# A feature-interaction tower on one core: a new order of whole and split groups, gathers in one row, low parts two groups later, first loads and dense features redone

## The reference

```python
x0 = xk = e
for idx, (W, b) in enumerate([(w0, b0), (w1, b1), (w2, b2)]):
    z = jnp.einsum('bhd,bkd,hks->bsd', x0, xk, W) + b[None, :, None]   # s = 128
    z = jax.nn.relu(z)
    if idx != 2:
        xk = z[:, :64, :]
        direct.append(z[:, 64:, :])
    else:
        direct.append(z)
logit = jnp.sum(jnp.concatenate(direct, axis=1), axis=-1)              # 512 x 256
h = jnp.concatenate([logit, dense_ctx], axis=1)
h = jnp.maximum(h @ W_top1 + b_top1, 0.0)                              # 272 -> 512
h = jnp.maximum(h @ W_top2 + b_top2, 0.0)                              # 512 -> 256
y = h @ W_top3
```

## Time and profile before

| | us |
|---|---|
| median of 3 runs | 640.83 (639.80 to 641.92) |
| profiled execution, its own time | 640.96 |
| its span, first to last instruction | 639.2 |
| mean granted TensorE clock | 0.992 |
| TensorE busy | 608.4 (95%) |
| VectorE busy | 551.1 (86%) |
| ScalarE busy | 302.9 (47%) |
| GpSimd busy | 462.2 (72%) |
| share of the last-ending chain on TensorE | 91% |

### The profile page before, as it was taken

The page is one execution under the profiler, slowest core; times in us unless marked ns, Lnnn a source line. Parts: engine busy times, 40 slices in busy tenths (PEclk is TensorE's granted clock), DMA queues, the critical chain, the costliest instruction groups (busy, mean ns, idle before and its releaser), DMA issues.

```text
span 639.2 us, 7262 instructions
## 1 busy us (share of the span) xinstructions
PE 608.4 (95%) x1938; PEld 364.9 (57%) x1938; DVE 551.1 (86%) x511; ACT 302.9 (47%) x374; POOL 462.2 (72%) x293
## 2 busy tenths in 40 slices
PE   0777999999999999999999999999999999999998
PEld 0334665656666665656666666656566666656463
DVE  1665999999999999999999999999999999999540
ACT  2124546445454545555464546465453545455313
POOL 6827787878878787878788787878788787547230
PEclk9997999999999999999999999999999999999998
DMA  7799697878869494958779594949688694922000
GB/s 252 161 230 221 139 209 153 197 159 188 170 141 219 102 215 95 223 116 202 148 163 201 120 218 99 218 101 218 133 188 165 146 214 97 218 51 70 2 0 0
DMA packets 28415, 98.46 MB, mean 154 GB/s; under 512 B 8017, under 2 KB 16977, under 8 KB 20082
## 3 DMA queue, kind: packets, MB, share of 16 engines
q1 hardware_dynamic: 21544, 93.68, 66.3%
q0 software_dynamic: 5120, 1.32, 1.9%
q10 hardware_dynamic: 1738, 3.33, 1.4%
HBM read 94.47 MB, written 3.84 MB: 154 GB/s over the span
## 4 chain that ended last, share of the span: by engine, by line
PE 91%; POOL 4%; DMA 3%; issue 1%; ACT 0%; SPq 0%; DVE 0%; ACTq 0%
PE z L614 42%; PE z L625 13%; PE z L620 13%; PE z L622 13%; PE z L604 4%; POOL gathered L411 3%; PE z L608 2%; PE z L607 2%; PE d_products L700 1%; DMA gathered<-in_tables,rows_sb 1%; DMA x_rows<-gathered 1%; PE z L675 1%; POOL low L352 0%; PE x_bank L675 0%; PE z L686 0%
## 5 line engine op out<-in xcount | busy, mean ns | idle before, releaser
L352 POOL TENSOR_TENSOR low<-products,high 128x1024 fp32r<-128x1024 f32 x128 | 303.8, 2390 | 110.9 <-ACT high L741 100.1
L465 DVE TENSOR_TENSOR products<-x_rep,xk 128x1024 f32<-128x1024 f32 (+1 forms) x258 | 333.3, 1339 | 24.3 <-ACT xk L725 16.6
L614 PE MATMUL z<-products,w_whole 128*128 128x512 f32 x640 | 296.9, 594 | 0.1
L741 ACT ACTIVATE high<-products 128x1024 fp32r<-128x1024 f32 x128 | 134.9, 1055 | 134.4 <-DVE products L465 121.8
L620 PE MATMUL z<-high,w_high 128*128 128x512 f32 x352 | 183.5, 521 | 6.8 <-ACT high L741 6.8
L411 POOL DMA_INDIRECT gathered<-in_tables,rows_sb x160 | 157.7, 985 | 44.3 <-issue 41.0
L614 PEld LDWEIGHTS z<-products,w_whole 128*128 128x128 f32 x640 | 121.5, 190 | 104.3 <-issue 92.8
L622 PE MATMUL z<-high,w_low 128*128 128x512 f32 x352 | 138.9, 395 | 0.0
L625 PE MATMUL z<-low,w_high 128*128 128x512 f32 x352 | 109.8, 393 | 1.8 <-POOL low L352 1.6
L620 PEld LDWEIGHTS z<-high,w_high 128*128 128x128 f32 x352 | 66.5, 189 | 45.6 <-issue 25.2
L622 PEld LDWEIGHTS z<-high,w_low 128*128 128x128 f32 x352 | 66.6, 189 | 37.0 <-issue 26.3
(11 more groups left out here) (51 smaller groups left out, 176.2 us busy)
## 6 DMA issues: line engine op xcount, KB each, us to landing
x_rep<-x_rows SPq DMA_DIRECT2D x60, 768.0 KB, 15.2
x_rep<-x_rows SPq DMA_DIRECT2D x66, 512.0 KB, 6.5
x_rows<-gathered SPq DMA_DIRECT2D x16, 225.0 KB
x_rep<-in_w ACTq DMA_DIRECT2D x2, 1280.0 KB, 9.6
gathered<-in_tables,rows_sb POOLq DMA_INDIRECT x160
x_rep<-x_rows SPq DMA_DIRECT2D x4, 384.0 KB, 6.3
x_same<-x_rows SPq DMA_DIRECT2D x15, 78.0 KB
x_same<-x_rows SPq DMA_DIRECT2D x16, 64.0 KB
```

The lines of the kernel that those rows point to most:

```text
L352: ops.tensor_tensor(low[0:p, slot, 0:n, :], product(index, p, n), high[0:p, slot, 0:n, :].bitcast(fp32), ALU.subtract).then_inc(low_by[kin ...
L465: nc.vector.tensor_tensor(slots, rep, row.unsqueeze(1).broadcast_to([p, n, N]), ALU.mult).then_inc(made, 1 + pair)
L614: mm = nc.tensor.matmul(out, w_whole[0:p, at, i, :], product(index, p, n)[:, i, :], start=(first and i == 0), stop=(last and i == n - 1))
L741: nc.scalar.activation(high[0:p, slot, 0:n, :], product(index, p, n), ACT.Copy).then_inc(rounded, 1)
```

## The change

- **Kinds.** `KINDS` becomes `ppwpdpwpdh` (layer 1), `wdws` (layer 0), `wwwwpwppwh` (layer 2). Per chunk there are as before 10 w, 8 p, 3 d, 2 h and 1 s. The slots' users follow: groups 0 and 1 now follow groups 19 (w) and 20 (p) in their ring slots, before 18 and 20 (both p); 2 and 3 follow 21 (p) and 22 (w).
- **Gathers.** All ten behind group 15, in layer 2 (before: one behind group 1, nine behind 6).
- **Low lag** 2 for 1.
- **ScalarE's order.** In chunk 0 the copy of x_same stands ahead of layer 0's groups, no longer ahead of group 2; the direct part of layer 2 comes one group later; xk1 (`after_layer1`) is made behind the rounding of groups 11 and 13, before behind that of 11 and 12. VectorE's reductions move by one group.
- **First loads.** Part (6, 10) is cut in two, SP no longer holds parts back until earlier ones have landed (`HELD`), and chunk 1's rows are written to DRAM, after a wait for their gathers, behind part 2 (`WRITTEN_AFTER`) instead of behind part 4. The tiles made by selection are chosen anew.
- **Dense features.** Instead of an fp32 product over 16 partitions, dense rows and their weights are loaded three times, at partitions 0, 32 and 64 of a tile pair that GpSimd has cleared; ScalarE rounds the pair into a free slot of `high`, VectorE puts the rests at partitions 64 and 32, and TensorE does one rounded pass over 128 partitions per block of 128 outputs. The last chunk's ScalarE gets two waits for it.

```diff
-FIRST_PARTS = [(4, 6), (0, 4), (6, 10), (10, 14), (14, 17), (17, T1)]
-SELECTED = [0, 1, 6, 2, 3]
+FIRST_PARTS = [(4, 6), (0, 4), (6, 8), (8, 10), (10, 14), (14, 17), (17, T1)]
+SELECTED = [0, 1, 2, 3, 6]
...
-KINDS = {1: "wpwpwppwdh", 0: "wsdw", 2: "wwpwpdpwph"}
+KINDS = {1: "ppwpdpwpdh", 0: "wdws", 2: "wwwwpwppwh"}
...
-GATHERS = {1: 1, 6: 9}
+GATHERS = {15: 10}
-LOW_LAG = 1
-SEL_SLOT = 0
+LOW_LAG = 2
+SEL_SLOT = 7
...
-        HELD = 3
-        WRITTEN_AFTER = 4
+        WRITTEN_AFTER = 2
...
             for q in range(1, len(FIRST_PARTS)):
-                if q >= HELD:
-                    sp.wait_ge(first_loaded[q - 2], 32)
                 for e in range(2):
                     load_replicated(sp, 0, e, FIRST_PARTS[q], first_loaded[q])
...
+            sp.wait_ge(dense_zeroed, 1)
+            for p in (0, 32, 64):
+                sp.dma_start(dense_rows[p:p + DENSE, 0, :], dense).then_inc(dense_loaded, 16)
+                sp.dma_start(dense_rows[p:p + DENSE, 1, :], wt1[256:256 + DENSE, :]).then_inc(dense_loaded, 16)
...
+                    if index == DENSE_TO and c == C - 2:
+                        pool.wait_ge(made, count("all", c, N1 + N0 + 1))
+                        nc.gpsimd.memset(dense_rows, 0.0).then_inc(dense_zeroed, 1)
...
+            def make_dense():
+                dve.wait_ge(dense_rounded, 1)
+                for i, p in ((0, 64), (1, 32)):
+                    nc.vector.tensor_tensor(dense_parts[p:p + DENSE, i, :], dense_rows[p:p + DENSE, i, :],
+                                            dense_parts[p:p + DENSE, i, :].bitcast(fp32),
+                                            ALU.subtract).then_inc(dense_made, 1)
...
-                nc.tensor.matmul(z_hidden1[m][:, :], wt1d_sb[:, m * 128:(m + 1) * 128], dense_sb,
+                nc.tensor.matmul(z_hidden1[m][:, :], dense_parts[:, 1, m * 128:(m + 1) * 128], dense_parts[:, 0, :],
                                  start=True, stop=False)
...
-                    if index == 2 and not last:
+                    if index == (N1 if first else 2) and not last:
                         copy_same(c + 1)
-                    if index == 3 and not first:
+                    if index == 4 and not first:
                         after_layer2(c - 1, first=isinstance(c, int) and c == 1)
+                    if last and index == N1:
+                        act.wait_ge(dense_loaded, 16 * 6)
+                        act.wait_ge(used, count("all", c, DENSE_FROM))
+                        nc.scalar.activation(dense_parts, dense_rows, ACT.Copy).then_inc(dense_rounded, 1)
-                    if index == N1 + 3:
+                    if index == N1 + 5:
                         after_layer1(c)
```

More of the change, by code:

```diff
@@ L234, in dlrm_cin_kernel @@
         wt1_sb = x0_rep[:, 0:2, 0:H1]
-        wt1d_sb = x0_rep[0:DENSE, 2, 0:H1]
-        dense_sb = x0_rep[0:DENSE, 3, 0:B]
+        dense_rows = x0_rep[:, 2:4, :]
+        dense_slot = next(SPLIT.index(i) % PART_RING for i in SPLIT if i in LAYER0)
+        same_slot = [i for i in SPLIT if SPLIT.index(i) % PART_RING == dense_slot and i not in LAYER0]
+        DENSE_FROM, DENSE_TO = max(i for i in same_slot if i < N1), min(i for i in same_slot if i > N1)
+        dense_parts = high[:, dense_slot, :, :]
         wt2_sb = x0_rep[:, 4:8, 0:H2]
@@ L270, in dlrm_cin_kernel @@
         top_loaded = sem("top_loaded")
+        dense_zeroed, dense_loaded = sem("dense_zeroed"), sem("dense_loaded")
+        dense_rounded, dense_made = sem("dense_rounded"), sem("dense_made")
         same_loaded = sem("same_loaded")
@@ L395, in _ @@
                         load_replicated(sp, c, e, part, rep_loaded[q])
+            sp.wait_ge(dense_zeroed, 1)
+            for p in (0, 32, 64):
+                sp.dma_start(dense_rows[p:p + DENSE, 0, :], dense).then_inc(dense_loaded, 16)
+                sp.dma_start(dense_rows[p:p + DENSE, 1, :], wt1[256:256 + DENSE, :]).then_inc(dense_loaded, 16)
             sp.wait_ge(made, count("all", C - 2, len(BODY) - 1))
-            sp.dma_start(dense_sb, dense).then_inc(top_loaded, 16)
             sp.dma_start(wt1_sb, wt1[0:256, :].rearrange("(t p) m -> p t m", p=128)).then_inc(top_loaded, 16)
-            sp.dma_start(wt1d_sb, wt1[256:256 + DENSE, :]).then_inc(top_loaded, 16)
             sp.dma_start(wt2_sb, wt2.rearrange("(t p) m -> p t m", p=128)).then_inc(top_loaded, 16)
@@ L533, in body @@
                             make_low(*late.pop(0))
+                        if isinstance(c, int) and c == C - 1:
+                            make_dense()
                         dve.wait_ge(xk1_ready, c + 1)
@@ L549, in body @@
                         make_low(*late.pop(0))
-                    if index == 8 and not (isinstance(c, int) and c == 0):
+                    if index == 9 and not (isinstance(c, int) and c == 0):
                         logits2(c - 1)
-                    if index == N1 + N0 + 3:
+                    if index == N1 + N0 + 2:
                         logits01(c)
@@ L678, in _ @@
             before_last, of_last = slice(0, B - BC), slice(B - BC, B)
-            pe.wait_ge(top_loaded, 16 * 5)
+            pe.wait_ge(top_loaded, 16 * 3)
+            pe.wait_ge(dense_made, 2)
             pe.wait_ge(direct0_ready, C)
@@ L783, in body @@
                         after_layer0(c)
+                    if last and index == DENSE_TO:
+                        act.wait_ge(used, count("all", c, N1 + N0))
                     if index in SPLIT + STACKS and not (last and index in LAYER0):
```

## The result

The change made the kernel slower: 649.03 us (median of 4 runs, 645.79 to 649.38) against 640.74 before (4 runs beside them), a ratio of 1.0118 (95% interval 1.0084 to 1.0152). The forecast was 644.7, so the sign and the place were right and the size was half of it; the median lies at the upper edge of the range, 0.03 above it. The profiled execution has a span of 647.6 us, 8.4 more than before.

The account below looks back on a forecast made before the run. TensorE was taken to bound the kernel, never waiting from 70 to 575 us. 639.2 - 1.8 (first chunk) + 7.8 (ring waits) + 0.7 (composition) - 2.8 (end) = 643.1 us span, 644.7 on the median; range 639.5 to 649.

Parts of the forecast that it names:

- The ring of product buffers: Steady chunks: TensorE waits for group 1's low part behind the double product of 0 and 1; 0.56, taken as 0.60 us.
- the 0.04 saved: Steady chunks: TensorE changes between fp32 and rounded operands less often, eight runs for ten, 0.04 us less per chunk.
- The two sides: From TensorE's start on group 19: it wants group 1's low part after 9.81 us, which is there after 10.37.
- The second ring: Groups 2 and 3 wait for TensorE's 22; the path sums to 36.0 us against 35.48, 0.5 to 0.6 over.
- The first chunk: Head: x_same block gone, DMA late next, layer 2 at 64.5 for 66.30; gain 1.8 us, ends 3.5 and -0.5.
- The rival of a cold first chunk: Head: TensorE waits some 4 us, low clock kept into layer 0, loss of about 0.9, 647.4 us; chance 0.16.
- The end: Dense features: four fp32 products of 1.05 us become rounded passes of 0.23; 2.8 us saved, between 2.5 and 3.3.
- The composition term: Layer 2 has two more whole groups and two fewer split, run once more than layer 1: +0.7 us.
- What was put at zero: Cost 0: ten gathers in one row, low lag of two; covered or early: GpSimd's clearing and dense loads.
- the rule weighed in the prediction: GpSimd shares SBUF interfaces with VectorE; a stacked low part could be up to 1.9 us longer per chunk, sum unchanged.
- the rival on the other side: Steady chunks: ring waits don't reach TensorE, only savings are left, -4.5, so 636.3 us; chance 0.14.

Follow-up runs that it names:

- e1: Changed kernel with groups 0 and 1 made as two products again, groups 2 and 3 still one double product: 644.04 us, ratio 1.0032 to the kernel before.
- e2: Changed kernel with no double product, groups 0 to 3 made one by one: 636.83 us, ratio 0.9920 to the kernel before.
- e9: Changed kernel with only groups 2 and 3 made one by one, 0 and 1 still one double product: 649.34 us, ratio 1.0141 to the kernel before.
- e12: Changed kernel with no double product and chunk 1's write after 14 of 20 tiles, no parts held: 632.27 us, ratio 0.9880 to the kernel before.
- e11: Kernel before with only the dense features redone and ScalarE's copy of x_same behind layer 1: 635.95 us, ratio 0.9918.
- e4: Kernel before with only the dense features redone: 639.77 us, ratio 0.9957.
- e10: Kernel before with only the gathers in one row in layer 2 and the low parts two groups later: 641.13 us, ratio 1.0007.
- e8: Kernel before with only the first loads as changed and the copy of x_same behind layer 1: 641.80 us, ratio 1.0023.
- e3: Changed kernel with the group order of before in the three layers and the selector slot of before: 649.87 us, ratio 1.0116 to the kernel before.
- e5: Changed kernel with the old group order and selector slot, and xk1 and direct2 at their old places in ScalarE's list: 642.32 us, ratio 1.0028.

## Why the prediction was half right

**The ring of product buffers: right in mechanism, too small in size.** Everything the forecast said would show is there: VectorE's double products wait for TensorE twice a chunk (26 waits, up to 1.3 us), TensorE waits for GpSimd's low part of 1 once a chunk, and e1, e2 and e9 come out as two rings would have it. The step that failed is the wait of 0.60 a chunk (0.56 by the first sum), measured 0.85; less the 0.04 saved, that is 0.81. The two sides were 9.81 and 10.37. TensorE was due at 9.79 (150.61 to 160.40), as reckoned. The low part came to it at 161.12, 10.51 after 150.61: 0.07 more from TensorE to VectorE (2.20 for 2.13), 0.03 to ScalarE, 0.05 back to TensorE. The first was set too small, the other two were named and left at zero. That makes a wait of 0.72. The rest is what a wait costs beyond itself; timeline of TensorE and its weight loads, the low passes of 0, not waiting, and of 1, waiting:

```profile
158.81 0.42 PEld L642 LDWEIGHTS z<-low,w_high 128*128 128x128 f32 x2
159.04 0.62 PE L642 MATMUL z<-low,w_high 128*128 128x512 f32 x2
159.49 0.39 PE L637 MATMUL z<-high,w_high 128*128 128x512 f32 x1
...
161.12 0.30 PEld L642 LDWEIGHTS z<-low,w_high 128*128 128x128 f32 x2 [0.99 <-POOL low L357]
161.12 0.74 PE L642 MATMUL z<-low,w_high 128*128 128x512 f32 x2 [0.56 <-POOL low L357]
161.71 0.59 PE L631 MATMUL z<-products,w_whole 128*128 128x512 f32 x1
```

What follows the two low passes starts after 0.45 in the first case (0.46 where it is a whole group, 150.15 to 150.61) and after 0.59 in the second. The weight load began 0.23 ahead of its pass in the first case, under the pass before, and together with it in the second. 0.72 + 0.13 = 0.85. And the wait comes 15 times, not 14: chunk 1 has it too. 15 x 0.85 - 14 x 0.04 = 12.2 us against the 7.8 of the sum, 4.4 more. The whole miss is 4.5 (8.4 of span for 3.9). Two other terms were off as well, the first chunk by +1.5 and the end by -1.2; that these nearly cancel is luck.

**The second ring** was worked out at 36.0 and is 36.09 when alone. That two rings agreed was taken as a reason to trust the size. It was none: both sums left out the handover to ScalarE and the restart. The first, which binds, was 0.29 short (0.85 for 0.56), the second 0.1.

**The first chunk: the gain did not come.** Forecast -1.8, measured -0.3 on TensorE (66.32 against 66.30 on VectorE). The wait for x_same is gone (the copy at 55.12 waits for nothing), the gathers landed within 34 to 36 (34.47), the rounding of 13 and xk1 took their 2.1. The step that failed is "12 tiles at 224 GB/s behind the gathers": it took the queue as full at that moment, and it had run dry. 2.9 us of transfer were lost in 30 to 38 us, 1.7 of them from 34 on, which is what layer 1's last tiles came late. Layer 1's last tiles were used at 52.20, not 50.5, group 12 at 62.55, not 60.5. e12 gives back 4 us.

**The rival of a cold first chunk came in beside it.** TensorE waited 4.46 us for the low part of 8 (forecast: some 4), and the granted clock was twice for some us at the lower of its two levels, 1.2 GHz (0.68, then 0.53 and 0.62 as means over 4 us); windows, columns as in the earlier trace rows:

```profile
42.00:46.00 4.00, 4.00 (x11) 2.69 (x10) 0.71 (x2) 1.38 (x2) 4.00 (x2) 0.68 1.00 234
58.00:62.00 4.00, 1.74 (x3) 1.16 (x4) 3.97 (x4) 0.00 (x0) 3.14 (x3) 0.53 1.09 250
62.00:66.00 4.00, 4.00 (x9) 2.05 (x7) 3.48 (x5) 2.56 (x4) 3.04 (x4) 0.62 1.00 218
...
635.00:640.00 5.00, 5.00 (x9) 1.98 (x9) 0.00 (x0) 1.42 (x3) 0.00 (x0) 0.66 0.00 0
```

In the first chunk it cost less than its price, since VectorE waited for tiles anyway: layer 2 began no later than before. The Trainium skill (TensorE: Matmul & The Clock Gate, the two states), which made this rival the likelier, agrees with the 4.46 us of waiting ahead of the second drop.

**The end** was forecast at -2.8 and is -4.0 in the chain, beyond its bound of 3.3 (e11's profile agrees with 4.0; the medians of e4 give less, for the reasons said there). The step took each dense pass as 0.23 and put the saving between 0.62 and 0.82 each; it is 0.81 for the pass and 0.20 more in the products behind it, which the text did not count. The composition term, +0.7, is +0.7.

**What was put at zero** held. Ten gathers in a row and the later low parts cost nothing (e10), GpSimd's clearing and the dense loads do not show in the chain. Stacked low parts on VectorE were 0.69 us in the steady part, so the contention with GpSimd that the rule weighed in the prediction speaks of did not occur there, as reckoned.

**Why the rival on the other side fell.** It wanted TensorE to have several tenths in hand behind the ring. It had less than nothing: 9.79 against 10.51.

## What to carry to other kernels

When a reorder changes which engine frees a buffer, walk from that release to the next use by the same engine and put down every handover and the restart of the waiting engine; left out or set too small, they were a third of the loss here. When an experiment gives less than its part of the trace promises, look in its own profile for what it lost elsewhere: e4 and e8 each hid a second effect of 1.7 us or more. A double-size instruction saves issue time on an engine that has slack and lengthens every ring it stands in; taking it apart here turned 1.2% slower into 0.8% faster, 12 us, of which the clock at the end may be 1.7. Ahead of a wait on a queue that carries the loads, queue enough to outlast the wait.

## What the runs showed of the hardware

- A wait of TensorE in front of a rounded pass cost 0.13 us beyond the wait, since the weight load is then not hidden.
- The 16 products of the second perceptron layer took 8.83 us before and as changed, with a granted clock of 0.66 from 635 to 640 us as changed, and 7.13 in e9 and e12, where it was 1.00. Nearly the same kernel falls on either side, so 1.7 us of spread between executions can come from this alone. The 645.79 among the runs has a mean clock of 0.997, the other three 0.989, so it may be such a one; it has no profile, and it is more than 1.7 faster.
- Four fp32 products got 0.20 us shorter when the 16-row fp32 product ahead of them became a rounded one of 128 rows.
- ScalarE started xk0 later than TensorE's records of group 13 explain: 2.7 us behind them in every chunk of e3, up to 3.0 in e5, 1.9 in e4 and once 3.4 in e2, where the kernel before has 0.94 and the one as changed 0.2. No view here shows why.
